# Transposes at the end of a step, scores at its beginning, in a non-local attention block on one core

## The chip, the core and the metric

The kernel runs on one core of a Trainium2 chip. Its time is the device time of one execution in microseconds (us). The engines of the core work at the same time, each through its own list of instructions in the order in which it is written, and meet only through semaphores: TensorE (PE in the rows, PEld for its weight loads), VectorE (DVE), ScalarE (ACT), GpSimd (POOL) and SyncE (SP), which issues the transfers.

## What is computed

The reference is a non-local attention block on x of shape 8 x 128 x 32 x 32, in float32: 8 images of 1024 positions with 128 channels, 64 inner channels.

```python
g     = einsum('bchw,oc->bhwo', x, w_g) + b_g            # (B, N, 64)
theta = einsum('bchw,oc->bhwo', x, w_theta) + b_theta    # (B, N, 64)
phi   = einsum('bchw,oc->bohw', x, w_phi) + b_phi        # (B, 64, N)
att   = softmax(einsum('bnc,bcm->bnm', theta, phi), axis=-1)
y     = einsum('bnm,bmc->bnc', att, g)
out   = einsum('bhwc,oc->bohw', y, w_out) + b_out
return x + out * inv + (bn_beta - bn_mean * inv)         # inv = bn_gamma / sqrt(bn_var + eps)
```

## The kernel before

The work is cut into 64 tiles of 128 positions, 8 of an image, and written as steps: in step k every engine does what is due then, for several tiles at different stages. With j = k mod 8 (the place in the image), step k holds the scores of tile k+1 (TensorE, `scores`, four matmuls into one of two PSUM buffers), the row maximum of tile k+1 (VectorE), the exponential of tile k (ScalarE, into one of four `probs` buffers), and for tile k-2 the turning of the probabilities: eight transposes on TensorE into `ps_flip`, in two halves of four; a high part in fp16 taken from each half by ScalarE (`high_parts`, into `pt_hi`); and the rest as a low part by VectorE (`low_parts`, into `pt_lo`). Only the places 0, 2, 3, 4 and 6 are turned so; the tiles of places 1, 5 and 7 are split by GpSimd and turned by DMA transposes. There is one `ps_flip` buffer for each half, so a half's transposes wait until the low part of the half before has been read out.

Four tiles make a half image of 512 columns. Its product with g is summed in `ps_y`: the high parts in the step of j = 7 (first half) or of j = 3 of the next image (second half), `sum_high`; the low parts two steps later, `sum_low`, at j = 1 and j = 5. In the step after that, j = 2 or 6, VectorE scales `ps_y` into `y_norm` (`scale_y`, the first thing that it does in that step) and TensorE multiplies it by w_out (`convolve`, one fp32 matmul that the rows show as two). VectorE adds the residual one step later. The rest of TensorE's steps: the projections of the next image at j = 0 and 1 (L844), g of the next image at j = 4 (`project_g`, L727), whose result ScalarE copies to `g_raw` at j = 5, and at j = 7 a transpose that spreads the peak of g (`spread_peak`, L749), which VectorE reads back with `read_peak` at j = 0 and without which the projection at j = 0 may not overwrite the bank.

Steps 0 to 7 are written out, steps 8 to 55 are three turns of a loop of two images, and steps 56 to 67 are written out again. The four tiles of the last half image are all turned by TensorE, after GpSimd has divided their rows by their sums. Nothing but the order of the code sets the order on an engine. In this order TensorE's step was: transposes of tile k-2; `sum_high`; scores of tile k+1; `sum_low`; projections, `convolve` or `project_g`; `spread_peak`. On ScalarE the high parts of tile k-2 came before the exponential of tile k, and on VectorE the low parts of tile k-2 before the maximum of tile k+1, but for j = 0.

Of the kernel before, what the change touches and what calls it, by code (L numbers as in the profile page):

```python
# [23 lines left out]
def build_nonlocal_attention(nc, x, w_tp_t, w_g_t, w_out_t, channel_vectors, out):  # L24
# [16 lines left out]
    P = 128  # L41
    BANK = 512
# [5 lines left out]
    MT = N // P  # L48
# [23 lines left out]
    with ExitStack() as ctx:  # L72
# [129 lines left out]
        def tile_at(it, k):  # L202
            return it * STEPS + k
# [4 lines left out]
        def image_at(it, k):  # L208
            return it * (STEPS // MT) + k // MT

        def exists(index, count):
            return not isinstance(index, int) or 0 <= index < count
# [272 lines left out]
        def _(act):  # L485
# [38 lines left out]
            def exponential(it, k):  # L524
                t = tile_at(it, k)
                if exists(t, TILES):
                    act.wait_ge(max_ready, t + 1)
                    if by_dma(it, k - PROB_RING):
                        wait(act, p_lo_ready, move_at(it, k - PROB_RING) + 1)
                    else:  # L530
                        wait(act, flipped, 2 * flip_at(it, k - PROB_RING) + 2)
                    nc.scalar.activation(probs[k % PROB_RING][:, :], ps_scores[k % 2][:, :], ACT.Exp,  # L532
                                         bias=neg_max[:, k % STEPS:k % STEPS + 1],
                                         accum_out=row_sum[:, k % STEPS:k % STEPS + 1]).then_inc(probs_ready, 1)

            def step(it, k):
                image, j = image_at(it, k), k % MT

                if j in (1, 2) and exists(image + 1, B):
                    c = j - 1  # L540
                    act.wait_ge(proj_ready, 2 * image + c + 1)
                    wait(act, lo_ready, 2 * image)
                    nc.scalar.activation(qk[:, c * BANK:(c + 1) * BANK], ps_misc[:, :], ACT.Identity,  # L543
                                         bias=BIAS_TP).then_inc(proj_out, 1)

                if j == 5 and exists(image + 1, B):
                    act.wait_ge(g_ready, image + 2)
                    evacuate_g(image + 1, ps_misc[:, :], g_raw[(k // MT + 1) % 2][:, :, :].rearrange("p t c -> p (t c)"))

                if j == 0:  # L550
                    exponential(it, k)
                high_parts(it, k)
                if j != 0:
                    exponential(it, k)

            run_steps(act, step)
            act.wait_ge(conv_ready, HALVES - 1)
# [4 lines left out]
        def _(dve):  # L562
# [79 lines left out]
            def next_maximum(it, k):  # L642
                if exists(tile_at(it, k + 1), TILES):
                    row_maximum(it, k + 1)

            def step(it, k):
# [60 lines left out]
                                                   scalar=g_factor[:, 0:1], in1=g_parts[0][:, :, 0:CI],  # L707
                                                   op0=ALU.mult, op1=ALU.subtract).then_inc(g_split, 1)

                if j == 0:  # L710
                    next_maximum(it, k)
                low_parts(it, k)
                if j != 0:
                    next_maximum(it, k)

            run_steps(dve, step)
            dve.wait_ge(resid_ready, B)
# [5 lines left out]
        def _(pe):  # L723
# [65 lines left out]
                             start=True, stop=True).then_inc(g_bias_ready, 1)  # L789
            pe.wait_ge(ident_ready, 1)  # L790

            def step(it, k):
                image, j = image_at(it, k), k % MT

                t = tile_at(it, k - 2)
                if exists(t, TILES) and not by_dma(it, k - 2):
                    f = flip_at(it, k - 2)
                    if in_last_half(t):
                        pe.wait_ge(probs_scaled, t - LAST_HALF + 1)
                    else:  # L800
                        pe.wait_ge(probs_ready, t + 1)
                    for c in range(2):
                        if isinstance(f, int) and f == 0:
                            pe.wait_ge(*((g_out, 1), (shift_ready, 1))[c])
                        wait(pe, pt_lo_ready, 2 * f + c - 1)
                        for a in range(HALF_TILES):
                            m = c * HALF_TILES + a
                            last = nc.tensor.transpose(ps_flip[c][:, a * P:(a + 1) * P],  # L808
                                                       probs[(k - 2) % PROB_RING][:, m * P:(m + 1) * P],
                                                       ident[:, :])  # L810
                        last.then_inc(flipped, 1)

                h, quarter = half_at(it, k - 6), (k - 6) % HALF_TILES
                ring, r = ring_of(k - 6), (k - 6) // MT % 2
                if quarter == 1 and exists(h, HALVES - 2):
                    pe.wait_ge(pt_lo_ready, 2 * flip_at(it, k - 7 + HALF_TILES))
                    pe.wait_ge(hi_moved[ring], moved_by(it, k - 6))
                    pe.wait_ge(g_split, image_at(it, k - 6) + 1)
                    wait(pe, y_scaled, h)
                    sum_high(ring, r, ps_y, slice(0, BANK), slice(0, BANK))  # L820
# [2 lines left out]
                if exists(t, TILES):  # L823
                    scores(t, it, k + 1)

                if quarter == 3 and exists(h, HALVES - 2):
                    pe.wait_ge(lo_moved[ring], moved_by(it, k - 6))
                    sum_low(ring, r, ps_y, slice(0, BANK), slice(0, BANK))

# [25 lines left out]
                if j == 4 and more:  # L855
                    pe.wait_ge(proj_out, 2 * image + 2)
                    wait(pe, result_ready, 2 * image - 1)
                    project_g(ps_misc, (k // MT + 1) % 2, range(MT)).then_inc(g_ready, 1)


                if tile_is(it, k, 1):
                    spread_peak(0, 0, ps_y[:, 0:P])
# [58 lines left out]
```

## Time and profile before

| | us |
|---|---|
| median of 3 runs (207.2 to 209.19) | 208.36 |
| the profiled execution | 208.85 |
| its span, in which the rows lie | 207.0 |
| one of the last two loop turns (two images) | 46.36, 46.11 |
| before the loop, and after it | 34.20, 34.20 |

The span runs from the first to the last instruction of the profiled execution. A start in a row is counted from the beginning of the span; busy time of TensorE has modelled ends, because its matmuls overlap.

### The profile page before, as it was taken

The page shows a single profiled execution, that of the slowest core. Times are in us where ns is not written, and L with a number is a line of the kernel's source. Part 1 is how long each engine was busy: PE and PEld are TensorE (multiplying, and loading weights), DVE is VectorE, ACT ScalarE, POOL GpSimd, SP SyncE. Part 2 cuts the span into 40 slices and gives each one's busy share as a digit, 9 for nine tenths or more (in the row PEclk, how much of TensorE's full clock was granted, in tenths as well). Part 3 has the DMA queues.
Part 4 walks back from the last instruction along what each step waited for, and adds up shares of the span by engine and source line. Part 5 has one row for each costly group of instructions (what it writes and reads, how often), then busy time and mean ns, then how long its engine had stood idle before and what let it go on. Part 6 is the DMA issues. An engine that isn't in the chain of part 4 may idle for free.

```text
span 207.0 us, 3966 instructions
## 1 busy us (share of the span) xinstructions
PE 195.8 (95%) x1100; PEld 133.6 (65%) x1100; DVE 176.9 (85%) x291; ACT 136.5 (66%) x245; POOL 152.4 (74%) x127
## 2 busy tenths in 40 slices
PE   7998879899999999999999999999999999899993
PEld 6576747567576946667566956677566956466542
DVE  0679896988999798988998898988998899989861
ACT  2866866846587674866577666866577766668621
POOL 2447898499787999699987999699988965944400
PEclk9999999999999999999999999999999999999999
DMA  5205997899999999899869997899888997929111
GB/s 152 96 22 164 228 99 150 126 285 206 191 138 248 230 164 178 210 276 237 159 152 257 229 190 186 183 255 228 146 177 183 221 161 176 156 47 141 65 43 62
DMA packets 59500, 35.28 MB, mean 170 GB/s; under 512 B 50400, under 2 KB 50912, under 8 KB 59488
## 3 DMA queue, kind: packets, MB, share of 16 engines
q1 hardware_dynamic: 59200, 35.01, 81.4%
q10 hardware_dynamic: 288, 0.14, 0.2%
q14 instruction: 7, 0.06, 0.2%
q8 instruction: 5, 0.08, 0.2%
HBM read 8.36 MB, written 4.23 MB: 61 GB/s over the span
## 4 chain that ended last, share of the span: by engine, by line
PE 69%; DVE 19%; issue 5%; ACT 2%; DMA 2%; DVEq 0%; ACTq 0%
PE ps_scores L743 20%; PE ps_flip L808 12%; PE ps_y L755 12%; DVE neg_max L599 7%; PE ps_misc L769 6%; DVE pt_lo L637 6%; PE ps_misc L727 6%; PE ps_y L762 5%; PE ps_misc L844 4%; DVE y_norm L616 3%; PE ps_scores L781 2%; DMA w_tp<-w_tp_t_dram 2%; ACT pt_hi L519 1%; PE ps_flip L727 1%; DVE inv_sum L664 1%
## 5 line engine op out<-in xcount | busy, mean ns | idle before, releaser
L532 ACT ACTIVATE probs<-ps_scores,neg_max 128x1024 f32<-128x1024 f32 x64 | 71.7, 1121 | 33.7 <-DVE neg_max L599 16.5
L599 DVE TENSOR_REDUCE neg_max<-ps_scores 128x1 f32<-128x1024 f32 x64 | 78.0, 1219 | 11.1 <-PE ps_scores L743 10.6
L637 DVE SCALAR_TENSOR_TENSOR pt_lo<-ps_flip,pt_hi 128x512 f16<-128x512 f32 x84 | 54.0, 685 | 5.0 <-ACT pt_hi L519 5.0
L519 ACT ACTIVATE pt_hi<-ps_flip 128x512 f16<-128x512 f32 x84 | 45.6, 595 | 13.4 <-PE ps_flip L808 13.4
L426 POOL TENSOR_TENSOR p_lo<-probs,p_hi 128x1024 f16<-128x1024 f32 x22 | 47.1, 2141 | 4.3 <-POOL p_hi L422 3.1
L743 PE MATMUL ps_scores<-phi_hh,theta_hl 128*128 128x512 f32 x128 | 46.5, 444 | 2.1 <-ACT probs L532 2.0
L808 PE MATMUL ps_flip<-ident,probs 128*128 128x128 f32 x336 | 44.8, 276 | 1.1 <-DVE pt_lo L637 0.7
L808 PEld LDWEIGHTS ps_flip<-ident,probs 128*128 128x128 f32 x336 | 37.6, 142 | 9.9 <-issue 3.5
L743 PE MATMUL ps_scores<-phi_ll,theta_hl 128*128 128x512 f32 x128 | 40.1, 394 | 0.0
L755 PE MATMUL ps_y<-pt_hi,g_parts 128*128 128x512 f16 (+1 forms) x128 | 29.8, 376 | 1.5 <-DVE pt_lo L637 1.3
L422 POOL TENSOR_SCALAR p_hi<-probs 128x1024 f16<-128x1024 f32 x22 | 23.6, 1072 | 7.6 <-ACT probs L532 7.1
L743 PEld LDWEIGHTS ps_scores<-phi_ll,theta_hl 128*128 128x128 f32 x128 | 24.0, 188 | 5.6
L755 PEld LDWEIGHTS ps_y<-pt_hi,g_parts 128*128 128x128 f16 x128 | 12.4, 98 | 21.1 <-issue 6.9
L743 PEld LDWEIGHTS ps_scores<-phi_hh,theta_hl 128*128 128x128 f32 x128 | 20.7, 190 | 6.3 <-ACT probs L532 3.8
L469 POOL TENSOR_TENSOR x_lo<-x_in,x_hi 128x512 fp32r<-128x512 f32 x14 | 17.9, 1284 | 0.8
L407 POOL TENSOR_TENSOR lo<-qk,hi 128x512 fp32r<-128x512 f32 x14 | 17.6, 1276 | 0.8
L769 PE MATMUL ps_misc<-y_norm,wout 128*128 128x512 f32 x30 | 16.3, 624 | 1.9 <-DVE y_norm L616 1.9
L616 DVE SCALAR_TENSOR_TENSOR y_norm<-ps_y,y_unit,inv_all 128x512 f32<-128x512 f32 x15 | 17.1, 1141 | 0.0
L762 PE MATMUL ps_y<-pt_lo,g_parts 128*64 128x512 f16 (+1 forms) x128 | 16.7, 382 | 0.0
L402 POOL TENSOR_SCALAR hi<-qk 128x1024 fp32r<-128x1024 f32 x7 | 7.4, 1052 | 12.3 <-ACT qk L543 12.3
L727 PEld LDWEIGHTS ps_misc<-wg,x_in 128*128 128x128 f32 x112 | 13.6, 191 | 0.6
L727 PE MATMUL ps_misc<-wg,x_in 128*128 128x64 f32 x112 | 13.2, 271 | 0.0
(80 smaller groups left out, 176.2 us busy)
## 6 DMA issues: line engine op xcount, KB each, us to landing
x_in<-x_in_dram SPq DMA_DIRECT2D x16, 256.0 KB, 3.3
inv_all<-inv_row SPq DMA_DIRECT2D x15, 256.0 KB, 4.2
out_dram<-resid SPq DMA_DIRECT2D x15, 256.0 KB, 2.5
phi_hh<-hi SPq DMA_DIRECT2D x14, 256.0 KB, 5.1
phi_ll<-lo SPq DMA_DIRECT2D x14, 256.0 KB, 5.3
theta_hl<-hi SPq DMA_DIRECT2D x7, 256.0 KB, 4.4
theta_hl<-lo SPq DMA_DIRECT2D x7, 256.0 KB, 5.0
pt_hi<-p_hi SPq DMA_TRANSPOSE x22, 4.3
```

The costliest lines, as they stand in the source:

```text
L422: nc.gpsimd.tensor_scalar(out=high[:, :], in0=p[:, :], scalar1=1.0, scalar2=0.0, op0=ALU.mult, op1=ALU.add).then_inc(p_hi_ready, 1)
L426: nc.gpsimd.tensor_tensor(low[:, :], p[:, :], high[:, :], ALU.subtract).then_inc(p_lo_ready, 1)
L519: nc.scalar.activation(pt_hi[ring][:, c * HALF_TILES:(c + 1) * HALF_TILES, slot * P:(slot + 1) * P], ps_flip[c][:, :].rearrange("p (a n) - ...
L532: nc.scalar.activation(probs[k % PROB_RING][:, :], ps_scores[k % 2][:, :], ACT.Exp, bias=neg_max[:, k % STEPS:k % STEPS + 1], accum_out=ro ...
L599: nc.vector.tensor_reduce(out=top, in_=ps_scores[k % 2][:, :], op=ALU.max, axis=AX.X, negate=True).then_inc(row_max_ready if by_dma(it, k) ...
L637: nc.vector.scalar_tensor_tensor(out=pt_lo[ring][where], in0=ps_flip[c][:, :].rearrange("p (a n) -> p a n", n=P), scalar=PROB_SCALE, in1=p ...
L727: last = nc.tensor.matmul(target[:, m * CI:(m + 1) * CI], x_in[r][:, m * P:(m + 1) * P], wg[:, :], start=True, stop=True)
L743: last = nc.tensor.matmul(ps_scores[k % 2][:, cc], theta_hl[r][:, cols], phi[:, cc], start=(n == 0), stop=(n == 1))
L755: nc.tensor.matmul(target[:, to], g_parts[r][:, m, :], pt_hi[ring][:, m, cols], start=(m == 0), stop=False, skip_group_check=True)
L762: last = nc.tensor.matmul(target[side * CI:(side + 1) * CI, to], g_parts[r][:, m, 0:CI], pt_lo[ring][:, m, cols], start=False, stop=(m >= ...
L769: nc.tensor.matmul(target, wout[:, 0:C], y_norm[:, cols], start=True, stop=True).then_inc(conv_ready, 1)
L808: last = nc.tensor.transpose(ps_flip[c][:, a * P:(a + 1) * P], probs[(k - 2) % PROB_RING][:, m * P:(m + 1) * P], ident[:, :])
```

## The change

TensorE's transposes of tile k-2 are moved from the beginning of step k to its end, behind the projections, `convolve` and `project_g`; a step now begins with `sum_high`, where it has one, and the scores. The `sum_low` of j = 5 moves with them, behind the transposes; that of j = 1 stays, since place 7 has none. `sum_high` waits for high parts where it waited for low parts, and `sum_low` takes over the wait for the low parts. ScalarE now takes the exponential of tile k ahead of the high parts of tile k-2 in every step, and VectorE the maximum of tile k+1 ahead of the low parts of tile k-2.

```diff
@@ ScalarE, step
-                if j == 0:
-                    exponential(it, k)
+                exponential(it, k)
                 high_parts(it, k)
-                if j != 0:
-                    exponential(it, k)
@@ VectorE, step
-                if j == 0:
-                    next_maximum(it, k)
+                next_maximum(it, k)
                 low_parts(it, k)
-                if j != 0:
-                    next_maximum(it, k)
@@ TensorE
-            def step(it, k):
-                image, j = image_at(it, k), k % MT
-
-                t = tile_at(it, k - 2)
...
+            def transposes(it, k):
+                t = tile_at(it, k)
...
+            def step(it, k):
+                image, j = image_at(it, k), k % MT
 
                 h, quarter = half_at(it, k - 6), (k - 6) % HALF_TILES
...
-                    pe.wait_ge(pt_lo_ready, 2 * flip_at(it, k - 7 + HALF_TILES))
+                    pe.wait_ge(pt_hi_ready, 2 * flip_at(it, k - 7 + HALF_TILES))
...
-                if quarter == 3 and exists(h, HALVES - 2):
+                if quarter == 3 and by_dma(it, k - 2) and exists(h, HALVES - 2):
+                    pe.wait_ge(pt_lo_ready, 2 * flip_at(it, k - 9 + HALF_TILES))
                     pe.wait_ge(lo_moved[ring], moved_by(it, k - 6))
                     sum_low(ring, r, ps_y, slice(0, BANK), slice(0, BANK))
...
+                transposes(it, k - 2)
+                h = half_at(it, k - 6)
+                if quarter == 3 and not by_dma(it, k - 2) and exists(h, HALVES - 2):
+                    pe.wait_ge(pt_lo_ready, 2 * flip_at(it, k - 9 + HALF_TILES))
+                    pe.wait_ge(lo_moved[ring], moved_by(it, k - 6))
+                    sum_low(ring, r, ps_y, slice(0, BANK), slice(0, BANK))
+
                 if tile_is(it, k, 1):
                     spread_peak(0, 0, ps_y[:, 0:P])
```

TensorE in the loop, from `project_g` at j = 4 to `sum_high` at j = 7, before (`probs2`, `probs3` and `probs0` hold the tiles of places 2, 3 and 4; a `ps_flip1` row is the second half of a tile's transposes, a `phi_ll` row the second half of a tile's scores):

```order
L727 MATMUL ps_misc<-wg,x_in0 128x64 x8
...
L808 MATMUL ps_flip1<-ident,probs3 128x128 x4
...
L743 MATMUL ps_scores0<-phi_ll1,theta_hl1 128x512 x2
L762 MATMUL ps_y<-pt_lo1,g_parts0 64x512 x8
...
L808 MATMUL ps_flip1<-ident,probs0 128x128 x4
...
L743 MATMUL ps_scores1<-phi_ll1,theta_hl1 128x512 x2
...
L769 MATMUL ps_misc<-y_norm,wout 128x512
...
L755 MATMUL ps_y<-pt_hi0,g_parts1 128x512 x8
```

The same stretch after:

```order
L721 MATMUL ps_misc<-wg,x_in0 128x64 x8
...
L800 MATMUL ps_flip1<-ident,probs2 128x128 x4
...
L737 MATMUL ps_scores0<-phi_ll1,theta_hl1 128x512 x2
...
L800 MATMUL ps_flip1<-ident,probs3 128x128 x4
L756 MATMUL ps_y<-pt_lo1,g_parts0 64x512 x8
...
L737 MATMUL ps_scores1<-phi_ll1,theta_hl1 128x512 x2
...
L763 MATMUL ps_misc<-y_norm,wout 128x512
...
L800 MATMUL ps_flip1<-ident,probs0 128x128 x4
...
L749 MATMUL ps_y<-pt_hi0,g_parts1 128x512 x8
```

The transposes of place 2 moved behind `project_g`, those of place 3 behind the scores, and those of place 4 behind the matmul with w_out (L769, now L763), so that five groups stand between `project_g` and that matmul as before, but other ones.

ScalarE at the same place, before (`probs0` is written by the exponential of place 4, `probs1` by that of place 5):

```order
L532 ACTIVATE probs0,row_sum<-ps_scores0,neg_max 128x1024
L547 REGISTER_ALU
L488 ACTIVATE g_raw0<-ps_misc 128x512
L518 ISA
L519 ACTIVATE pt_hi0<-ps_flip0 128x4x128
L518 REGISTER_ALU
L519 ACTIVATE pt_hi0<-ps_flip1 128x4x128
L527 REGISTER_ALU
...
L532 ACTIVATE probs1,row_sum<-ps_scores1,neg_max 128x1024
```

And after:

```order
L519 ACTIVATE pt_hi0<-ps_flip1 128x4x128
L547 REGISTER_ALU
L488 ACTIVATE g_raw0<-ps_misc 128x512
L527 REGISTER_ALU
L217 REGISTER_ALU
L532 ACTIVATE probs1,row_sum<-ps_scores1,neg_max 128x1024
L518 ISA
L519 ACTIVATE pt_hi0<-ps_flip0 128x4x128
```

The first row of the second piece is the high part of place 2, the last that of place 3: between them stand now both the copy of g and the exponential of place 5, of which only the copy stood ahead of the high part of place 3 before.

TensorE in the last steps, from the last `sum_low` of a loop-like step to the last `sum_high` but one (`probs0` and `probs1` hold tiles 60 and 61), before:

```order
L762 MATMUL ps_y<-pt_lo1,g_parts0 64x512 x8
L808 MATMUL ps_flip0<-ident,probs0 128x128 x4
L808 MATMUL ps_flip1<-ident,probs0 128x128 x4
L743 MATMUL ps_scores1<-phi_hh1,theta_hl1 128x512 x2
L743 MATMUL ps_scores1<-phi_ll1,theta_hl1 128x512 x2
L769 MATMUL ps_misc<-y_norm,wout 128x512
L808 MATMUL ps_flip0<-ident,probs1 128x128 x4
L808 MATMUL ps_flip1<-ident,probs1 128x128 x4
L755 MATMUL ps_y<-pt_hi0,g_parts1 128x512 x8
```

And after:

```order
L756 MATMUL ps_y<-pt_lo1,g_parts0 64x512 x8
L737 MATMUL ps_scores1<-phi_hh1,theta_hl1 128x512 x2
L737 MATMUL ps_scores1<-phi_ll1,theta_hl1 128x512 x2
L763 MATMUL ps_misc<-y_norm,wout 128x512
L800 MATMUL ps_flip0<-ident,probs0 128x128 x4
L800 MATMUL ps_flip1<-ident,probs0 128x128 x4
L800 MATMUL ps_flip0<-ident,probs1 128x128 x4
L800 MATMUL ps_flip1<-ident,probs1 128x128 x4
L749 MATMUL ps_y<-pt_hi0,g_parts1 128x512 x8
```

The transposes of tile 60 moved behind the matmul with w_out and stand directly ahead of those of tile 61.

## Rows read from the trace of the kernel before

**Rows 1.** The page: busy us, share of the span and instructions of each engine.

```profile
PE 195.8 (95%) x1100; PEld 133.6 (65%) x1100; DVE 176.9 (85%) x291; ACT 136.5 (66%) x245; POOL 152.4 (74%) x127
```

**Rows 2.** Windows: second loop turn, and steps after the loop.

```profile
core 0: us, PE busy (x) PEld busy (x) DVE busy (x) ACT busy (x) POOL busy (x), PEclk, DMA share, GB/s
...
80.33:126.69 46.36, 46.05 (x263) 31.72 (x263) 42.51 (x69) 32.11 (x58) 40.47 (x33) 1.00 0.95 212
...
172.80:207.00 34.20, 28.81 (x175) 17.64 (x174) 26.16 (x45) 18.95 (x36) 14.48 (x12) 1.00 0.45 92
```

**Rows 3.** Chain that ended last, one image: start us, us, what ran.

```profile
92.96 1.73 PE ps_misc L727 x16
94.69 0.88 PE ps_flip L808 x8
95.57 0.93 PE ps_scores L743 x4
96.50 0.98 PE ps_y L762 x8
97.49 1.02 PE ps_flip L808 x8
98.51 0.94 PE ps_scores L743 x4
99.45 1.05 PE ps_misc L769 x2
...
103.17 0.32 PE ps_misc L749
103.50 0.88 PE ps_flip L808 x8
...
105.30 0.69 PE ps_misc L844 x3
...
110.59 0.86 PE ps_misc L769 x2
...
115.90 1.74 PE ps_misc L727 x16
```

**Rows 4.** Timeline, ScalarE, VectorE and a weight load at j = 5 and 6.

```profile
94.73 0.60 ACT L488 ACTIVATE g_raw<-ps_misc 128x512 f32<-128x512 f32 x1 [0.92 <-PE ps_misc L727]
...
95.22 1.08 ACT L519 ACTIVATE pt_hi<-ps_flip 128x512 f16<-128x512 f32 x2
...
95.85 1.29 DVE L637 SCALAR_TENSOR_TENSOR pt_lo<-ps_flip,pt_hi 128x512 f16<-128x512 f32 x2 [0.58 <-ACT pt_hi L519]
...
96.18 1.13 ACT L532 ACTIVATE probs<-ps_scores,neg_max 128x1024 f32<-128x1024 f32 x1
...
97.05 1.21 DVE L599 TENSOR_REDUCE neg_max<-ps_scores 128x1 f32<-128x1024 f32 x1
...
98.18 1.14 DVE L616 SCALAR_TENSOR_TENSOR y_norm<-ps_y,y_unit,inv_all 128x512 f32<-128x512 f32 x1
...
99.37 0.30 PEld L769 LDWEIGHTS ps_misc<-y_norm,wout 128*128 128x128 f32 x2 [0.37 <-DVE y_norm L616]
```

**Rows 5.** Timeline at j = 0 of the second loop turn, ScalarE and VectorE.

```profile
81.21 0.28 DVE L593 TENSOR_REDUCE g_peak_all<-ps_misc 128x1 f32<-128x128 f32 x1
...
81.43 1.12 ACT L532 ACTIVATE probs<-ps_scores,neg_max 128x1024 f32<-128x1024 f32 x1 [1.20 <-PE ps_flip L808]
...
82.38 1.22 DVE L599 TENSOR_REDUCE neg_max<-ps_scores 128x1 f32<-128x1024 f32 x1 [0.30 <-PE ps_scores L743]
...
82.54 1.07 ACT L519 ACTIVATE pt_hi<-ps_flip 128x512 f16<-128x512 f32 x2
...
83.78 1.29 DVE L637 SCALAR_TENSOR_TENSOR pt_lo<-ps_flip,pt_hi 128x512 f16<-128x512 f32 x2
```

**Rows 6.** Timeline, TensorE, matmul with w_out at j = 6 of the last image.

```profile
191.05 1.10 PE L769 MATMUL ps_misc<-y_norm,wout 128*128 128x512 f32 x2 [0.21 <-DVE y_norm L616]
```

**Rows 7.** Timeline, TensorE, first `sum_high`, in step 7, before the loop.

```profile
29.91 1.89 PE L755 MATMUL ps_y<-pt_hi,g_parts 128*128 128x512 f16 x8 [1.31 <-DVE pt_lo L637]
```

More of the change, by code:

```diff
@@ L790, in _ @@
             pe.wait_ge(ident_ready, 1)
-            def step(it, k):
-                image, j = image_at(it, k), k % MT
-                t = tile_at(it, k - 2)
-                if exists(t, TILES) and not by_dma(it, k - 2):
-                    f = flip_at(it, k - 2)
+            def transposes(it, k):
+                t = tile_at(it, k)
+                if exists(t, TILES) and not by_dma(it, k):
+                    f = flip_at(it, k)
                     if in_last_half(t):
@@ L808, in step @@
                             last = nc.tensor.transpose(ps_flip[c][:, a * P:(a + 1) * P],
-                                                       probs[(k - 2) % PROB_RING][:, m * P:(m + 1) * P],
+                                                       probs[(k) % PROB_RING][:, m * P:(m + 1) * P],
                                                        ident[:, :])
                         last.then_inc(flipped, 1)
+            def step(it, k):
+                image, j = image_at(it, k), k % MT
                 h, quarter = half_at(it, k - 6), (k - 6) % HALF_TILES
```

## The prediction

> **What bounds the kernel now.** I read the page first: TensorE is busy for 195.8 of 207.0 us, VectorE for 85% of the span [rows 1]. Next the windows: in a loop turn TensorE is busy for 46.05 of 46.36 us and VectorE for 42.51; after the loop TensorE is busy for 28.81 of 34.20 us [rows 2]. A modelled end can hide waits, so the third view decides: in the chain of waits one image of the loop is one unbroken string of TensorE groups [rows 3]. The reader should see two things there. Most groups of a kind take the same time (0.88 for a tile's transposes, 0.93 for scores, 0.98 for `sum_low`, 0.86 for the matmul with w_out), so TensorE runs through its list without a stop; and the exceptions are small: 1.02 for the transposes of place 4, 1.05 for the w_out matmul of j = 6. From the end of `project_g` (94.69) to the end of the peak's transpose (103.50, where the next group starts) it is 8.81 us, and from there to the end of the next `project_g` (115.90 + 1.74 = 117.64) 14.14 us, together 22.95 for an image; a turn of 46.36 is twice that and 0.46 at the loop's branch [rows 2, 3]. In the loop TensorE's list is the bound, with VectorE 8% behind it; after it the two alternate.
>
> The Trainium skill ("Perfetto Trace Analysis", section "Identifying the Most-Contended Engine") warns against matmul busy time as a measure and takes the share of weight loads instead. That is 31.72 of 46.36 us here, so by the page a third of a turn would be open to a better order. No row of this image shows such room: its groups stand back to back.
>
> **The change part by part.** No matmul, reduction or activation is added or taken away; only places in the lists move. So the list of TensorE costs the same, and the question is where it now has to wait. I follow the results through the three engines, in times after the end of `project_g`. A hand-over from engine to engine takes 0.04 (end of `project_g` 94.69, start of its copy 94.73 [rows 3, 4]).
>
> *The w_out matmul of j = 6.* Before, it stood behind the transposes of place 3, scores, `sum_low`, transposes of place 4, scores, and began at 99.45 with 0.19 of wait in it (1.05 against 0.86). After, it stands behind the transposes of place 2, scores, transposes of place 3, `sum_low`, scores: 0.88 + 0.93 + 0.88 + 0.98 + 0.94 = 4.61 of work, the same amount. But its input `y_norm` is VectorE's next work after the low parts of place 3, and these now come later against TensorE:
> - the first half of the transposes of place 2 is done at 0.44 (half of 0.88); ScalarE's high parts of place 2 start at 0.48;
> - they keep ScalarE for 0.96 (95.22 to 96.18 [rows 4]); at 1.44 it copies g, for 0.49 (94.73 to 95.22), to 1.93;
> - the exponential of place 5, now ahead of the high parts of place 3, takes 1.11 (81.43 to 82.54 [rows 5]), to 3.04, though the transposes of place 3 had put out their first half long before;
> - the low parts start 0.63 after the high parts (95.22 to 95.85 [rows 4]), at 3.67, and VectorE goes on 1.20 later (95.85 to 97.05), at 4.87, with `y_norm`;
> - the weight load with `y_norm` starts 1.19 after its start (98.18 to 99.37), at 6.06.
>
> So TensorE would wait 6.06 - 4.61 = 1.45 us. If ScalarE were no hindrance, VectorE's list alone gives 0.48 + 0.63 + 1.20 (low, place 2) + 1.13 (maximum, 97.05 to 98.18) + 1.20 (low, place 3) + 1.19 = 5.83, nearly the same; these two are my bounds, and I take 6.06, because both orders are fixed in the lists. After that come 0.86, the transposes of place 4 (0.88), `sum_high` (1.73, like `project_g`), scores (0.93) and the peak (0.33): 10.79. Of this, 0.88 (place 2) stood ahead of `project_g` before, so 9.91 against 8.81: **1.10 us more for an image** (0.87 by the lower bound), six images in the loop.
>
> *The projection of j = 0 and the w_out matmul of j = 2.* Times from the end of the peak's transpose. Before, the latter began at 110.59 - 103.50 = 7.09; without the transposes of place 0, which now stand behind it, 6.21. After: VectorE's maximum of place 0 starts at -0.29 with the end of its scores, the peak is read at 0.84 (1.13 later) and known at 1.16 (0.28 and the hand-over [rows 5]), so the projection, behind only 0.93 of scores, waits 0.23 and ends at 1.85 (0.69 [rows 3]). High parts of place 6 start at 2.33 (0.44 + 0.04), low parts could at 2.96. VectorE's maximum of place 1 starts 1.17 - 0.30 = 0.87 after the reading of the peak (81.21 to 82.38, 0.30 of it wait [rows 5]), at 1.71, its low parts 1.40 later (82.38 to 83.78), at 3.11; 1.20 and 1.13 on, `y_norm` starts at 5.44 and the matmul at 6.63: 0.42 late. At the turn's branch TensorE loses 0.46 anyway and VectorE does not, so there it is nothing: **0.42 a turn**, between 0 and 0.84.
>
> A turn: 2 x 1.10 + 0.42 = 2.62; three turns: 7.9 us.
>
> *After the loop.* The last image goes the same way without `project_g`; the exponential of place 4 now stands ahead of the high parts of place 2 as that of place 5 did. Its w_out matmul of j = 6 waited 0.21 for `y_norm` already [rows 6], so I take 1.10 - 0.21 = 0.9. Then the transposes of tile 60, moved behind it, add their 0.88. And those of tile 61 directly behind them find `ps_flip` occupied: 0.44 + 0.04 + 0.63 + 0.65 (half of 1.29) = 1.76 until the first low half of tile 60 is out, 0.88 more than back to back. Sum **2.7** (0.9 if the last two are hidden, 3.3 if 61's second half is as late again).
>
> *Before the loop.* Image 0 has no w_out matmul. Its turned tiles may come up to 1.1 later, but the first `sum_high` is preceded by 1.31 us of idle time [rows 7]: nothing.
>
> *The other edits.* `sum_high` waiting for high parts is a weaker wait at a place without a stop in the loop (the group starts on time in [rows 3]): nothing. Maxima and exponentials come sooner at j = 2 and later at j = 5, and the scores that wait for them stand two tiles behind: nothing. If that cover were gone, the exponential of place 5 (1.11) would be the price for each image.
>
> Sum: 7.9 + 2.7 = 10.6 us. The profiled execution would take 208.85 + 10.6 = 219.4; it lay 0.5 above the median of the runs, so the prediction is 208.36 + 10.6 = 219.0. The bounds: down to 6 x 0.87 + 0 + 0.9 = 6.1 (214.5), up to 7.9 + 1.3 + 3.3 and 1.2 for new small stops (0.2 an image, of the size of the 0.19 at w_out) = 13.7 (222).
>
> **The rivals.** *Faster.* Scores first feed the longest chain (scores, maximum, exponential) early, so the small stops vanish: 0.14 at place 4 (1.02 - 0.88) and 0.19 at w_out, 0.33 an image, 2.0 in six, and about as much after the loop: 204.4, range 203 to 206.2. It decides at one point: `y_norm` of j = 6 must start no later than 4.61 - 1.19 = 3.42 after `project_g`, and even VectorE's list alone gives 4.64 (5.83 - 1.19). Only if VectorE took the low parts of place 2 before the end of `project_g` could it be so, and their transposes stand behind it.
>
> *No change.* TensorE's list is as long as before [rows 2, 3]; if the 1.45 of wait is paid back, because the other engines use it to run ahead and the rest of the image has the stops no more, it is 208.4, range 206.3 to 210.5. Against it: all TensorE groups after the wait are bare work.
>
> *Half of it.* The wait of j = 6 stands but shrinks as the loop settles, and the end hides its own: 7.9 / 2 = 4.0, so 212.4, range 210.5 to 214.5.
>
> *Worse.* The later exponential of place 5 also delays GpSimd (40.47 of 46.36 us busy) and its DMA transposes (DMA share 0.95 [rows 2]), so that `sum_high` of j = 3 waits as well, say another half of 1.10 an image: 219.0 + 3.3 = 222.3 and more.
>
> **How the numbers follow.** Forecast (214.5 to 222): 0.70. Half: 0.10. No change: 0.10. Faster: 0.06. Worse: 0.04. 219.0 is the forecast's own time. The range needs the forecast and the half case to hold 0.80: 210.5 to 222.5, the top a little up into the worse case. A measurement of this kernel can tell about 1% (2.1 us) from no change; faster by more than that 0.06, within it 0.11 (no change and the edge of the half case), slower 0.83.
>
> **What would show it.** After: the weight load of the w_out matmul at j = 6 idle for over 1 us until `y_norm`, in every image; the chain of waits in the loop leaves TensorE there for high parts, low parts and `y_norm`; the turns 48.5 to 49.5 us long; the projection of j = 0 waiting some 0.2 for the reading of the peak; the transposes of tile 61 idle for about 0.9. I am wrong if the turns stay at 46.4 or fall, which would mean that `y_norm` starts less than 3.5 us after `project_g`, or if the loss lies elsewhere, at `sum_high` of j = 3 above all.

## The result and the profile after

The changed kernel takes 227.76 us (median of 6 runs, 227.34 to 229.4), the kernel before 208.51 beside it (6 runs, 206.57 to 209.19): ratio 1.100, 95% interval 1.0939 to 1.1062. The direction was forecast, the size was not: 19.3 us more instead of 10.6, and outside the range. The profiled execution has a span of 227.5 us.

The page first, the row of each engine's busy time, with its share of the span and its instructions, and TensorE's granted clock in 40 slices:

```profile
PE 201.4 (89%) x1100; PEld 134.7 (59%) x1100; DVE 183.7 (81%) x291; ACT 137.4 (60%) x245; POOL 152.0 (67%) x127
...
PEclk9999999999999999999999999999999999699998
```

Against [rows 1] no instruction was added (1100, 291, 245, 127 as before), yet VectorE is busy for 6.8 us more: 183.7 against 176.9. An order cannot do that; some of its instructions must have become longer. That is the first thing to follow. TensorE's granted clock falls to 0.6 in one slice near the end and is 0.8 in the last; in the trace of the kernel before all forty slices are at 0.9 or more.

The windows: two images of the loop (from one `project_g` to the second after it, the length of a turn), then from the last peak's transpose to the end, then three stretches of the end:

```profile
core 0: us, PE busy (x) PEld busy (x) DVE busy (x) ACT busy (x) POOL busy (x), PEclk, DMA share, GB/s
71.29:123.39 52.10, 47.74 (x265) 31.75 (x264) 44.61 (x69) 32.52 (x58) 40.27 (x33) 1.00 0.88 183
187.75:227.50 39.75, 30.55 (x174) 18.66 (x172) 27.28 (x45) 18.76 (x34) 13.39 (x11) 0.94 0.35 74
...
192.00:194.00 2.00, 1.31 (x6) 0.67 (x4) 2.00 (x4) 0.88 (x3) 1.04 (x1) 1.00 1.05 200
194.00:196.00 2.00, 0.97 (x3) 0.44 (x3) 2.00 (x2) 1.12 (x2) 1.99 (x1) 0.79 0.81 119
196.00:198.00 2.00, 2.00 (x8) 1.38 (x7) 0.07 (x1) 0.00 (x1) 1.85 (x4) 0.50 1.15 165
```

A turn is 52.10 instead of 46.36 [rows 2], 5.7 more where 2.62 was forecast. Only 1.7 of it is busy time of TensorE (47.74 against 46.05); for the rest it stands idle. VectorE has 44.61 instead of 42.51, 2.1 more with the same 69 instructions.

The chain that ended last, one image, the answer to [rows 3]:

```profile
97.31 1.73 PE ps_misc L721 x16
99.04 0.46 PE ps_flip L800 x4
...
102.15 1.00 PE ps_y L756 x8
...
103.91 1.12 DVE y_norm L613
...
105.08 1.12 PE ps_misc L763 x2
...
108.80 0.94 PE ps_scores L737 x4
...
111.31 1.40 DVE inv_sum L661
...
112.97 1.19 DVE neg_max L596
...
116.72 1.06 DVE y_norm L613
...
117.83 1.12 PE ps_misc L763 x2
```

Before, this was an unbroken string of TensorE groups. Now it leaves TensorE twice in an image. The first time is the forecast one: after `project_g` (its end 97.31 + 1.73 = 99.04) through high parts, low parts and `y_norm` to the w_out matmul of j = 6, at 105.08. That is 6.04 after `project_g`; the forecast said 6.06. The second is at j = 0, and it holds a piece that the prediction never looked at: the scaling of `inv_sum`, a `tensor_scalar` on two columns, of 1.40 us.

The timeline at that place, VectorE (first four rows, the last of them the maximum of place 1), GpSimd (fifth) and TensorE (the last three, the first of them the peak's transpose). It answers to [rows 5]:

```profile
110.91 0.28 DVE L590 TENSOR_REDUCE g_peak_all<-ps_misc 128x1 f32<-128x128 f32 x1
111.11 0.17 DVE L657 RECIPROCAL inv_sum<-row_sum 128x4 f32<-128x4 f32 x1
111.31 1.40 DVE L661 TENSOR_SCALAR inv_sum<-inv_sum 128x2 f32<-128x2 f32 x1
...
112.93 1.22 DVE L596 TENSOR_REDUCE neg_max<-ps_scores 128x1 f32<-128x1024 f32 x1
...
110.55 2.13 POOL L426 TENSOR_TENSOR p_lo<-probs,p_hi 128x1024 f16<-128x1024 f32 x1 [0.29 <-DMA pt_lo<-p_lo]
...
109.57 0.27 PE L743 MATMUL ps_misc<-ident,g_peak 128*128 128x128 f32 x1
...
111.34 0.47 PE L840 MATMUL ps_misc<-x_hi,w_tp_hi 128*128 128x512 f32 x1 [0.56 <-DVE g_peak_all L590]
...
117.83 1.12 PE L763 MATMUL ps_misc<-y_norm,wout 128*128 128x512 f32 x2 [0.92 <-DVE y_norm L613]
```

The reader should compare two ends: VectorE's scaling ends at 111.31 + 1.40 = 112.71, GpSimd's low parts at 110.55 + 2.13 = 112.68. The scaling began inside the GpSimd instruction and ended with it. The reciprocal 0.2 us ahead of it, inside the same GpSimd instruction, took its usual 0.17. Of TensorE's rows the one at 111.34 is the projection behind its wait for the reading of the peak, a wait that the prediction expected, but with 0.23 instead of 0.56.

The same place in the trace of the kernel before, VectorE and GpSimd, rows that the prediction had not called on:

```profile
104.73 0.37 DVE L664 TENSOR_SCALAR inv_sum<-inv_sum 128x2 f32<-128x2 f32 x1
...
104.03 1.05 POOL L422 TENSOR_SCALAR p_hi<-probs 128x1024 f16<-128x1024 f32 x1 [0.17 <-issue]
105.37 2.15 POOL L426 TENSOR_TENSOR p_lo<-probs,p_hi 128x1024 f16<-128x1024 f32 x1 [0.29 <-POOL p_hi L422]
```

There the scaling met the end of GpSimd's high parts (105.08) and was long by 0.2 only. It has changed sides: it stood 0.64 ahead of the start of GpSimd's low parts, and now stands 0.76 behind it.

### The profile page after: what moved, and what is told of

Same layout as the page of the kernel before. It is cut to its first block, busy times and chain, and to the rows that moved or that the text cites. A ratio compares the mean times of both kernels' runs of the same rounds, so it can differ in the third digit from the quotient of the medians.

```text
span 227.5 us, 3980 instructions
## 1 busy us (share of the span) xinstructions
PE 201.4 (89%) x1100; PEld 134.7 (59%) x1100; DVE 183.7 (81%) x291; ACT 137.4 (60%) x245; POOL 152.0 (67%) x127
## 4 chain that ended last, share of the span: by engine, by line
PE 53%; DVE 28%; issue 10%; ACT 5%; DMA 2%; DVEq 1%; ACTq 0%
PE ps_flip L800 12%; PE ps_y L749 12%; PE ps_scores L737 11%; DVE neg_max L596 9%; PE ps_misc L763 8%; DVE y_norm L613 7%; PE ps_misc L721 5%; DVE pt_lo L634 4%; DVE inv_sum L661 4%; PE ps_y L756 3%; ACT pt_hi L519 2%; DMA vec<-vectors_dram 2%; DVE g_peak_all L590 1%; ACT probs L532 1%; DVE phi_ll L578 1%
## 5 line engine op out<-in xcount | busy, mean ns | idle before, releaser
L519 ACT ACTIVATE pt_hi<-ps_flip 128x512 f16<-128x512 f32 x84 | 46.0, 599 | 38.3 <-PE ps_flip L800 38.3
L800 PEld LDWEIGHTS ps_flip<-ident,probs 128*128 128x128 f32 x336 | 38.9, 144 | 17.4 <-issue 11.4
L800 PE MATMUL ps_flip<-ident,probs 128*128 128x128 f32 x336 | 46.3, 279 | 1.9 <-DVE pt_lo L634 1.1
L763 PE MATMUL ps_misc<-y_norm,wout 128*128 128x512 f32 x30 | 17.7, 672 | 12.3 <-DVE y_norm L613 12.3
L763 PEld LDWEIGHTS ps_misc<-y_norm,wout 128*128 128x128 f32 x30 | 4.6, 193 | 18.6 <-DVE y_norm L613 15.2
```

Source lines behind the costliest of these rows:

```text
L519: nc.scalar.activation(pt_hi[ring][:, c * HALF_TILES:(c + 1) * HALF_TILES, slot * P:(slot + 1) * P], ps_flip[c][:, :].rearrange("p (a n) - ...
L763: nc.tensor.matmul(target, wout[:, 0:C], y_norm[:, cols], start=True, stop=True).then_inc(conv_ready, 1)
```

## The experiments

Kernels that ran together shared a chip, and the kernel before ran there with them; ratios are to those runs. Where two kernels are compared in us, the medians of the kernel before were 206.5 to 206.8.

**E1, the changed kernel with the scaling split.** The same two columns, in two instructions:

```diff
-    moved = inv_sum[:, first:last + 1:2]
-    nc.vector.tensor_scalar(out=moved, in0=moved, ...)
+    for slot in IN_HALF[ring_of(k - 1)]:
+        moved = inv_sum[:, cols.start + slot:cols.start + slot + 1]
+        last = nc.vector.tensor_scalar(out=moved, in0=moved, ...)
+    last.then_inc(inv_sum_ready, 1)
```

Expected: 

> The changed kernel, but VectorE's scaling of two columns of inv_sum (one instruction of 128x2 at j = 0, 1.33 to 1.40 us long in the loop after the change, 0.17 before) is written as two instructions of one column; the one of j = 4 had one column already. Theory A: the instruction stood still until GpSimd's low part of place 7 had ended (111.31 + 1.40 = 112.71 against 110.55 + 2.13 = 112.68), and only the form with two columns does so, since the one-column form at 97.78 took 0.15 in the middle of such a GpSimd instruction (95.88 to 98.02). Then both pieces take 0.15 to 0.17, the w_out matmul of j = 2 comes about 1.1 earlier in every image, and 6 x 1.1 in the loop and some 0.8 behind it go: 220 us. Theory B: it is slow at this place for another reason (it follows its own reciprocal, or code is fetched there): the first of the two pieces then takes 1.3 again, and the time stays at 227 to 228.

Measured: 221.38 us (221.28 to 221.88), ratio 1.0704 (1.0607 to 1.0801). One instruction more in every image, and 6.4 us less; VectorE's busy time on the page is 176.8 us again. The timeline of VectorE and of GpSimd, at j = 0:

```profile
108.04 0.21 DVE L661 TENSOR_SCALAR inv_sum<-inv_sum 128x1 f32<-128x1 f32 x2
...
107.29 2.13 POOL L426 TENSOR_TENSOR p_lo<-probs,p_hi 128x1024 f16<-128x1024 f32 x1 [0.29 <-DMA pt_lo<-p_lo]
```

Both one-column instructions lie inside GpSimd's low parts and take 0.21 together. So the long scaling is a cause of its own, and what is left, 14.9 us (221.38 against 206.48 for the kernel before beside it), is nearer to what was forecast.

**E2, the kernel before with the same split.** Expected: 

> The kernel before with the same two one-column instructions. Theory A: only the first loop turn had the long form (34.30, 1.52 us); that one goes, and up to 1.3 us with it: 207 to 208.5. Theory B: nothing moves, 208.5.

Measured: 206.16 us (205.75 to 207.93), ratio 0.9993 (0.9949 to 1.0037). No gain: before, the instruction was short in most images, and where it was long the time does not show it. In the loop of the kernel before it mostly met the last 0.4 us of GpSimd's high parts or nothing, and there the two-column form is harmless.

**E7 and E8, the dose.** The kernel before with one more VectorE instruction an image, on a scratch tensor, behind the one-column scaling of j = 4, with two columns (E7, the diff) and with one (E8, 0:1 and 4:5):

```diff
+    if ring_of(k - 1) == 0:
+        nc.vector.tensor_scalar(out=dose[:, 0:2], in0=dose[:, 4:6], ...)
```

Expected of E7: 

> The kernel before with one more VectorE instruction in each image: a two-column tensor_scalar on a scratch tensor right behind the one-column scaling of inv_sum at j = 4, where GpSimd is 0.6 us into its low parts. Lock theory (a two-column tensor_scalar that starts inside a GpSimd instruction waits for that instruction's end, a one-column one doesn't): the added instruction takes 1.2 to 1.5 us where it would take 0.17, and the kernel takes 0.3 to 1.2 us more in each image, 209 to 215. Rival (the long instructions were long for another reason, a wait for the exponential's row sums or for the semaphore): it takes 0.17, time 206 to 208.

Expected of E8: 

> Control: the same added instruction at the same place with one column instead of two. Lock theory: 0.15 us long in every image, time within 1 us of the kernel before. Rival (any added VectorE instruction at this place costs): the same time as with two columns.

Measured: E7 211.61 us (210.66 to 212.08), ratio 1.0197 (1.011 to 1.0285); E8 206.63 (206.09 to 209.04), ratio 1.0019 (0.997 to 1.0068). VectorE and GpSimd in E7 at one of these places:

```profile
117.08 0.15 DVE L666 TENSOR_SCALAR inv_sum<-inv_sum 128x1 f32<-128x1 f32 x1
117.15 1.48 DVE L669 TENSOR_SCALAR dose<-dose 128x2 f32<-128x2 f32 x1
...
116.47 2.13 POOL L427 TENSOR_TENSOR p_lo<-probs,p_hi 128x1024 f16<-128x1024 f32 x1 [0.28 <-POOL p_hi L423]
```

Two instructions of one kind, one behind the other, inside one GpSimd instruction: one column 0.15, two columns 1.48, to the end of GpSimd's (118.63 and 118.60). The added ones of E8:

```profile
L669 DVE TENSOR_SCALAR dose<-dose x8: 144/144/145, 21.8 to 182.2; 128x1 f32<-128x1 f32 x8
```

The tensor was a scratch one that nobody waits for, so neither the row sums nor a semaphore can be the reason. Seven of E7's eight added instructions lie inside GpSimd's low parts, and all seven end with it; the eighth, with GpSimd idle, took 0.16. The cause of the long scaling is shown from both sides. So the opening's sentence that the engines meet only through semaphores is too strong: here VectorE waited for GpSimd without one.

**E6, transposes ahead of the w_out matmul alone.** E1, but in the steps j = 2 and j = 6 the transposes stand ahead of the matmul:

```diff
+    if j % HALF_TILES == 2:
+        transposes(it, k - 2)
     h = half_at(it, k - 10)
     if j % HALF_TILES == 2 and exists(h, HALVES - 2):
...
         convolve(h, ps_misc[:, :], slice(0, BANK))
...
-    transposes(it, k - 2)
+    if j % HALF_TILES != 2:
+        transposes(it, k - 2)
```

Expected: 

> The changed kernel with the split scaling, and with the transposes moved ahead of the w_out matmul in the steps j = 2 and j = 6 alone; all other steps keep them at the end. Theory (the wait for y_norm at these two places is the loss): the 0.88 of the transposes fills the wait at both places, the w_out matmuls wait 0.6 and 0 less than before or not at all, so 0.9 to 1.5 us less in each of six images, time 212 to 216 against 221.4 with the split alone. Rival (the wait is only moved: what holds TensorE is the chain of exponential, high parts and low parts, whatever stands ahead): 219 or more.

Measured: 212.71 us (212.55 to 213.51), ratio 1.0277 (1.019 to 1.0365): 8.7 less than E1. The chain of E6 at j = 2, then from j = 4 to 6:

```profile
110.24 0.87 PE ps_flip L801 x8
111.11 0.86 PE ps_misc L764 x2
...
119.13 1.25 PE ps_flip L801 x8
...
121.37 1.12 PE ps_scores L738 x4
122.49 0.87 PE ps_flip L801 x8
...
123.37 1.12 PE ps_misc L764 x2
```

At j = 2 the matmul is a bare 0.86 again. At j = 6 the transposes now fill the wait; what is left of stops there (1.25, 1.12 and 1.12 against 0.88, 0.93 and 0.86) is 0.8.

**E5, transposes directly behind scores.** E1, with the transposes of every step, and the `sum_low` of j = 5 behind them, moved from the step's end to the place behind its scores:

```diff
     if exists(t, TILES):
         scores(t, it, k + 1)
+    transposes(it, k - 2)
+    if quarter == 3 and not by_dma(it, k - 2) and exists(h, HALVES - 2):
...
+        sum_low(ring, r, ps_y, slice(0, BANK), slice(0, BANK))
...
-    transposes(it, k - 2)
-    if quarter == 3 and not by_dma(it, k - 2) and exists(h, HALVES - 2):
...
-        sum_low(ring, r, ps_y, slice(0, BANK), slice(0, BANK))
```

Expected: 

> The changed kernel with the two-column scaling of inv_sum written as two instructions of one column, and with the transposes (with the sum_low of j = 5 behind them) directly behind the scores of every step instead of at the step's end, so that they stand ahead of the projection, the w_out matmul and project_g again. Theory (what is left of the loss after the split is TensorE waiting at the projection of j = 0 and at the w_out matmuls of j = 2 and 6, because no transposes stand ahead of them any more; scores first and the new order on ScalarE and VectorE cost nothing themselves): TensorE's list runs without a stop again, an image 22.9 to 23.2 us, time 204 to 208. Rival (scores first, or the later exponential of place 5, holds TensorE somewhere else as well): an image stays at 24.3 or more, time 215 or more.

Measured: 207.04 us (206.59 to 209.34), against 206.84 of the kernel before: ratio 1.0016 (0.9983 to 1.0049). The chain of E5, one image from the peak's transpose on:

```profile
99.97 0.32 PE ps_misc L744
100.30 0.95 PE ps_scores L738 x4
101.24 0.87 PE ps_flip L801 x8
102.11 0.70 PE ps_misc L847 x3
...
106.55 0.87 PE ps_flip L801 x8
107.42 0.86 PE ps_misc L764 x2
108.28 1.73 PE ps_y L750 x8
...
112.71 1.75 PE ps_misc L722 x16
```

TensorE's string is whole again. So scores first costs nothing, the new order on ScalarE and VectorE costs nothing with it, and all of what E1 had left came from the transposes standing at the step's end, behind the projection, the w_out matmul and `project_g`.

**E3 and E4, the change in halves.** E3 has TensorE's new order with the old one on ScalarE and VectorE, E4 the reverse:

```diff
-    exponential(it, k)
+    if j == 0:
+        exponential(it, k)
     high_parts(it, k)
+    if j != 0:
+        exponential(it, k)
```

This is E3's edit of the changed kernel, the same with `next_maximum` and `low_parts` on VectorE; E4 undoes the same lines in the kernel before.

Expected of E3: 

> Only TensorE's part of the change; ScalarE and VectorE in the order of before. If the place of the transposes on TensorE is the cause, this is as slow as the whole change or slower: the maxima of places 5 and 6 now both stand between the low parts of place 2 and y_norm, by the rows 0.48 + 0.63 + 1.20 + 1.35 + 1.20 + 1.13 + 1.19 = 7.2 after project_g against 6.04 measured for the whole change, so 1.1 an image more, 234 us. The rival is that the order on ScalarE and VectorE is the cause (the exponential of place 5 ahead of the high parts of place 3): then this one is much nearer to the kernel before, 210 to 216.

Expected of E4: 

> Only ScalarE's and VectorE's part; TensorE in the order of before. If the place of the transposes is the cause, this costs less than half of the change: the high parts of place 3 stand behind the exponential of place 5, the transposes of place 4 wait for the low parts of place 3 until 3.63 and 4.27 after project_g, and the w_out matmul of j = 6 begins at 5.7 against 4.95: 0.7 an image, 1 to 2 after the loop, 214 us. By the rival (ScalarE and VectorE are the cause) it is near 227.

Measured: E3 268.35 us (four runs, 263.65 to 270.91; its mean TensorE clock was lower too, 0.949 to 0.974, so that no ratio is given), E4 227.97 (227.3 to 228.87), ratio 1.1009 (1.0903 to 1.1115). E3 is far above both of its expectations. E4 is far above the theory's 214 and lies where its rival put it, near 227; but with E3 as slow as it is, the rival, that the order on ScalarE and VectorE is the cause, can't be the whole of it either. In E3 the groups of ScalarE's high parts and of the weight loads for scores; behind the second bar stands the idle time and what ended it:

```profile
L519 ACT ACTIVATE pt_hi<-ps_flip 128x512 f16<-128x512 f32 x84 | 46.4, 595 | 92.6 <-PE ps_flip L806 92.6
...
L743 PEld LDWEIGHTS ps_scores<-phi_hh,theta_hl 128*128 128x128 f32 x128 | 20.3, 194 | 54.6 <-ACT probs L532 53.1 <-issue 0.6 <-DVE phi_ll L581 0.3
```

ScalarE waits 92.6 us for transposes, and TensorE 53.1 for exponentials: with the high parts ahead of the exponential on ScalarE, and the transposes behind the scores on TensorE, each step's exponential waits until TensorE has come to its end, and the scores two tiles on wait for that exponential. In E3, then, TensorE's new order needs the other half of the change. In E4 the group of the transposes, and the scaling of `inv_sum` at one place:

```profile
L802 PE MATMUL ps_flip<-ident,probs 128*128 128x128 f32 x336 | 47.9, 281 | 17.1 <-DVE pt_lo L634 16.5 <-issue 0.5
...
87.55 1.40 DVE L661 TENSOR_SCALAR inv_sum<-inv_sum 128x2 f32<-128x2 f32 x1
```

Here the transposes, ahead of the scores, wait 16.5 us for low parts that now stand behind the maximum, and the long scaling is there too, in every image; no run tells how much of E4's 21 us is the one and how much the other. So the long scaling is not bound to TensorE's new order: what counts is where VectorE is when GpSimd starts its low parts.

**E9, E10 and E11, the end of the kernel.** E9 splits the scaling outside the loop alone; E10 adds four matmuls of zeros in a wait of TensorE; E11 is the changed kernel once more, on their chip. The edit of E9:

```diff
+    for part in ([[s] for s in slots] if isinstance(it, int) else [slots]):
+        moved = inv_sum[:, cols.start + part[0]:cols.start + part[-1] + 1:2]
+        last = nc.vector.tensor_scalar(out=moved, in0=moved, ...)
```

and that of E10, in the last image:

```diff
     wait(pe, result_ready, h)
+    if j == 6:
+        for i in range(4):
+            nc.tensor.matmul(ps_misc[:, 0:P], warm[:, :], warm[:, :], start=True, stop=True)
     convolve(h, ps_misc[:, :], slice(0, BANK))
```

Expected of E9: 

> The changed kernel with the scaling of inv_sum split into one-column instructions outside the loop alone, so that the loop keeps its long two-column instructions and only the one behind the loop (0.93 us at 189.01) goes. Theory (the end's extra loss over the forecast is this instruction and, after it, 1.66 us in which TensorE ran at a lower granted clock because it had waited so long): the granted clock stays at 1.0 in the last 40 us, from the last peak's transpose to the end 37.0 to 37.7 us instead of 39.7, time 2 to 2.6 less than the changed kernel. Rival (the fall of the clock has nothing to do with it): 0.9 less, the clock falls again.

Expected of E10: 

> The changed kernel with four added TensorE matmuls (128x128 of zeros, into ps_misc, overwritten at once) ahead of the w_out matmul of j = 6 of the last image, where TensorE waits 1.03 us for y_norm before it runs at the lower granted clock. Nothing else differs, and the added work lies in a wait. Theory (the clock fell because TensorE had stood still): granted clock 1.0 there, the w_out matmul 1.1 or less and the transposes 0.9 (1.97 and 1.68 in the changed kernel), time 1 to 1.7 less. Rival (the clock falls anyway, or the wait of 1.03 alone isn't what it hangs on): clock 0.5 again, time the same or 0.3 more.

Expected of E11: 

> The changed kernel itself, unchanged, on the chip of the two runs beside it, so that a difference of 1 to 2 us can be told. Both theories: 226.5 to 228.5, and the two-column scaling 1.3 to 1.5 us long in the loop.

Measured: E9 226.86 us (226.74 to 228.24), E10 227.58 (227.21 to 231.19), E11 227.90 (227.5 to 229.93); ratios 1.0997 (1.095 to 1.1043), 1.1009 (1.0962 to 1.1057) and 1.1051 (1.0999 to 1.1102). E9 is 1.0 us shorter than E11 by the medians, and 0.7 by the last stretch of the traces (50.25 against 50.97): the long scaling behind the loop, 0.93, is 0.21 in two pieces, and nothing else went. The reason is E11 itself: in its profiled execution the clock did not fall. Its w_out matmul of j = 2 of the last image, and ahead of it the one of the first trace of the changed kernel:

```profile
195.07 1.97 PE L763 MATMUL ps_misc<-y_norm,wout 128*128 128x512 f32 x2 [1.03 <-DVE y_norm L613]
```

```profile
194.87 1.10 PE L763 MATMUL ps_misc<-y_norm,wout 128*128 128x512 f32 x2 [1.02 <-DVE y_norm L613]
```

The same wait, with and without the fall. E10's text names the wrong place: this matmul is that of j = 2, and the added matmuls of j = 6 ran from 206.9 on, 11 us later, in another wait, where 1.1 us of TensorE work cost nothing. So E10 says nothing of the clock.

## Why the prediction was wrong

Where the time went is best told by stretches between the starts of `project_g`. The changed kernel is taken from E11's trace, and beside the kernel before stands E8, which runs in its time:

| stretch, us | before | E8 | changed (E11) | E1 | E6 | E5 |
|---|---|---|---|---|---|---|
| start to `project_g` of image 0 | 22.62 | 22.11 | 20.86 | 20.92 | 20.78 | 21.66 |
| to that of the next image | 23.77 | 21.54 | 23.94 | 22.72 | 22.46 | 21.57 |
| five images more | 115.74 | 115.68 | 129.83 | 125.65 | 120.18 | 115.65 |
| to the end | 44.87 | 44.97 | 50.97 | 50.21 | 47.28 | 45.92 |
| span | 207.0 | 204.3 | 225.6 | 219.5 | 210.7 | 204.8 |

**The w_out matmul of j = 6: right in place and size.** It began 6.04 after `project_g`, forecast 6.06, in every image, and E6 and E5 give the time back when transposes fill or remove that wait.

**The projection of j = 0 and the w_out matmul of j = 2: the step that failed.** Their places were right: the projection waits for the reading of the peak, and the matmul for `y_norm`. But the sum took 0.87 from the reading of the peak to the maximum of place 1 out of one place of the kernel before [rows 5], and the trace there has the scaling of `inv_sum` in it at 0.17. In the changed kernel the scaling is 1.40 and the stretch 2.02 (110.91 to 112.93). From the reading to the matmul it is 6.92 (110.91 to 117.83), forecast 5.79 (6.63 - 0.84). That is 1.13 more, and the scaling alone is longer by 1.23; in E1, with the short scaling, the same stretch is 5.96 (107.64 to 113.60). The reading itself came 1.07 after the end of the peak's transpose (109.57 + 0.27 = 109.84), forecast 0.84. Why scaling and low parts now meet is argued, not shown: the peak comes 1.1 us later by the wait at j = 6, and VectorE's scaling, which follows the peak, comes later with it, while GpSimd's work hangs on an exponential taken earlier. E5 fits that: it has the new order on ScalarE and VectorE but no wait, and in four of its six loop images the scaling lies at the end of GpSimd's high parts, as before (101.50 in one of 100.61 to 101.66). E1 prices the long scaling: five images 129.83 against 125.65, 4.2 us, and 6.4 in the whole kernel. The prediction took GpSimd into account as an engine that is busy for so long, and not as one that another engine's instruction can be stopped by. A hint stood in the trace of the kernel before. The group of this line, minimum, median and maximum of its durations in ns:

```profile
L664 DVE TENSOR_SCALAR inv_sum<-inv_sum x15: 153/156/1520, 22.2 to 184.9; 128x1 f32<-128x1 f32 x8, 128x2 f32<-128x2 f32 x7
```

One of fifteen took ten times the median.

The Trainium skill has this rule, on the page "SBUF — State Buffer", section "Who interferes with whom": VectorE in its two-port modes and GpSimd share a port pair, the one that issues first keeps it for its whole instruction, and the other is blocked until then; `tensor_scalar` is among the operations that can enter such a mode. The trace agrees for two columns: in E7 1.48, with an end within 0.03 us of that of GpSimd's instruction. By the Trainium skill's page "VectorE: DVE Perf Modes", section "What auto-detection actually checks", an instruction with one source enters such a mode if source and destination lie in SBUF and their outermost non-unit dimensions are both even, or equal. Two columns meet that; for one column, which has no such dimension beside the partitions, the section doesn't say it, and here the one-column form took 0.15 and was never long. No run tried another number of columns.

**The price of a w_out matmul that waits: mis-sized.** The sum had 0.86 for the matmul behind the wait. Each that waited took 1.10 to 1.13, in the kernel before as well (1.10 in [rows 6]), and in E1 the one of j = 2, which came within 0.05 us of `y_norm`, took 1.12 too. In the rows its weight load no longer lies beside other matmuls: load and matmul both begin at 105.08 in the changed kernel, while at j = 2 of the kernel before the load began 0.16 ahead of the matmul (110.27 and 110.43 in the timeline), beside the scores. That this is the whole reason is argued. It is 0.26 for each, two an image, 2.6 in five images. With it the forecast for E1's five images is 6.55 (five halves of the 2.62 a turn) + 2.6 = 9.2, against 125.65 - 115.68 = 10.0 measured. Of what is left, the projection of j = 0 is a part: behind its wait it took 0.94 in E1's chain, where the sum had 0.69.

**After the loop: nearly right.** From the end of the last peak's transpose to the end it was 37.5 in E1 and 38.3 in E11, against 34.2 [rows 2]: 3.3 and 4.1, forecast 2.7. The long scaling, 0.93 against 0.21, is the difference between the two, as E9 shows. The first trace has 1.7 more than E11, with the fallen clock in it. The transposes of tile 61 waited 1.13, forecast 0.9.

**Before the loop: right, and a lesson.** The first `sum_high` began at 28.26 in E11 and at 29.91 in the kernel before [rows 7], which looks like 1.65 us gained. E8, in the old order, has it at 27.93: the profiled execution of the kernel before had a late first image (23.77 against 21.54 in E8), for a reason that was not followed. Against E8 nothing was gained there. It also says that the loss, against an execution without that, is 21.3 us (225.6 against 204.3).

**"The other edits: nothing": right as far as it went.** E5 keeps scores first, `sum_high` behind the high parts, and both exponential and maximum first, and costs 0.2 us in 207. But none of this was free by itself: E3 and E4 show that either half of the change, without the other, costs 10% or more (in E4 with the long scaling in it).

**The rivals.** Worse was given 0.04, with DMA transposes and `sum_high` as its mechanism. The time came out there, but not for that reason: `sum_high` shows no wait in the trace of the changed kernel. A rival in which one engine's instruction is lengthened by another engine's was missing. The reading against "faster" and "half" held: the wait at j = 6 was neither hidden nor paid back.

Two things stay open. The clock of TensorE fell near the end in the profiled execution of the changed kernel, and by its mean clock it fell in one more of its first six runs as well (0.989 and 0.99, 229.4 us each, against 227.3 to 228.0 of the others) and in one of E10's (0.99, 231.19 us), but in none of E11's; the wait ahead of it was the same in both traces, and E9 and E10 could not tell what decides it. And no version beat the kernel before: E5, the best in the new order, ties with it.

## What to carry to other kernels

When an order is changed, look not only at who waits for whom, but at what then runs beside what: an instruction of VectorE on a few bytes can take the rest of a GpSimd instruction, so a delay worked out for one engine has to be carried on to the next collision. Read the longest of a group's durations, not the mean: one of 1.52 us in a group with a median of 0.16 says that there is a hazard which another order may hit every time. And work whose input is long ready (here the transposes) belongs ahead of a matmul that waits; behind it, it covers nothing, and in these rows the matmul's own weight load comes into the open too.

## What was not expected of the hardware

A `tensor_scalar` of VectorE on 128x2 float32 in SBUF that began inside a GpSimd `tensor_tensor` lasted to within 0.04 us of that instruction's end: 0.93 to 1.59 us in the changed kernel, 0.67 to 1.82 in E7. Inside a GpSimd `tensor_scalar` it did the same (0.37 in the kernel before), and with GpSimd idle it took 0.16 to 0.17. The same with 128x1 took 0.14 to 0.16 in either place, and a `reciprocal` of 128x4 stayed at 0.17 inside the GpSimd instruction. TensorE's granted clock fell to 0.50 of full speed, its level of 1.2 GHz, in the stretch of 196 to 198 us, after it had been busy for 1.31 and 0.97 us in the two stretches of 2 us ahead; its w_out matmul took 1.97 us. In E11 the same stretches read:

```profile
192.00:194.00 2.00, 1.20 (x4) 0.67 (x4) 2.00 (x3) 0.88 (x3) 1.25 (x2) 1.00 1.53 181
194.00:196.00 2.00, 1.14 (x4) 0.64 (x5) 1.85 (x2) 0.92 (x2) 2.00 (x2) 1.00 0.78 159
196.00:198.00 2.00, 2.00 (x15) 1.28 (x14) 0.88 (x2) 1.50 (x3) 1.85 (x3) 1.00 0.87 127
```

There TensorE had about as little work, the clock stayed at 1.0 throughout, and the matmul took 1.10.
